# Mixture-of-experts and gated delta attention in one program: one merged head block, a store in steps, scanned counts, and the triangular inversion's 64x64 products interleaved one unit ahead

## The chip, the cores and the metric

The program runs on one core of one Trainium2 chip. The metric is the device time of one execution in microseconds. Everything is float32. Engines: PE (matrix products), PEld (its weight loads), DVE (vector), ACT (scalar), POOL (GpSimd), SP (the engine that issues most DMAs here). Each runs its own list of instructions in order and waits on semaphores.

## The reference

Eight sequences of 256 tokens with 256 features (T = 2048 tokens, 16 row tiles of 128) go through three residual parts. `norm` is a layer norm without weights.

```python
x = x + 0.5 * ffn(norm(x))     # router: softmax over 8 experts, 2 best; each expert 256 -> 896 -> 256,
                               # h = silu(x @ w1) * (x @ w3), out = h @ w2, mixed by the router's weights
x = x + attn(norm(x))
x = x + 0.5 * ffn(norm(x))

# attn: qkvz = x @ W_qkvz (16 key heads, 32 value heads, 128 wide); q, k, v through a causal
# convolution of 4 taps and silu; q and k of unit length; g = -exp(A_log)*softplus(a + dt_bias), beta = sigmoid(b)
def step(state, inp):
    qt, kt, vt, gt, bt = inp
    state = state * jnp.exp(gt)[..., None, None]
    pred = jnp.einsum('bhk,bhkv->bhv', kt, state)
    delta = (vt - pred) * bt[..., None]
    state = state + kt[..., None] * delta[..., None, :]
    return (state, jnp.einsum('bhk,bhkv->bhv', qt, state))
# then core * rsqrt(mean(core^2)) * norm_weight * silu(z), and @ W_out
```

## The kernel before

**Expert parts** (`build_ffn`, twice). `build_norm` makes the normalised rows and their transposes. A chain of small DVE instructions ranks the rows among the experts: `before` is the running count per expert, made by 16 additions one behind the other (L337), `base` the first tile of each expert, made by 8 more (L344). POOL then scatters 32 times 128 rows to `rows_in`, the expert matmuls run over 39 row tiles, and a last block gathers 32 times 128 rows from `rows_out` (POOL, L616) while DVE adds them to `x` (L627). `Pools.end_part` clears the part's semaphores on POOL in a block of its own; a block begins and ends with a barrier of all engines. `build_out` stores `x` (2 MB) with one DMA.

**Head of the attention.** `build_norm` again, then `attention_tables`: 32 small products with `W_ba` (L718; a product is two instructions in the trace, here and elsewhere), a `partition_broadcast` on POOL (L710), and a chain of DVE and ACT instructions that makes the decay tables. The weights of the first head are loaded when the block behind it begins (L1001 to L1004).

**The attention** is worked in 64 units: 16 key heads, and for each 4 units of two sequences (`idx(u)` counts them, `u[1]` is the place within the head). The linear recurrence is done in chunks of 128 tokens; each chunk needs the inverse of a 128x128 triangular matrix, for 8 (chunk, value head) pairs in a unit. Its 32x32 diagonal blocks are inverted on DVE for a whole head at once (`blocks`, in 16 pieces over 4 units), stored to DRAM by `blocks_out` (L1076) and loaded back by `load_c` and `load_t`. The rest is done on PE: `inv_x(32)` and `inv_n` with 32x32 products (L1226, L1227, L1240 to L1242), `inv_x(64)` with eight 64x64 products (L1230) into `inv_bank[0]`, partitions 64 to 127, and `inv_last` with eight (L1250) into `inv_bank[1]`, partitions 0 to 63. ACT copies the result to `invT`, which `solve` reads.

`walk` writes the program of each engine out: it runs over iterations i from -11 to 66, and in each over the steps in the order of a table by hand (one for the filling, one for the steady stretch, one for the draining). A step works on unit i + `STAGE[step]`, so that a unit's steps lie up to 14 iterations apart: projections of q and k at 11, `turn`, `products`, `scan`, `mix` and `spill` at 10, `blocks` at 5, `blocks_out` and the projections of v and z at 1, the inversion at 0, `solve` and `state` at -1, the output at -3. The filling table holds while no v is projected (10 iterations), the draining one when no q and k are left to project (14).

`blocks` piece 0 of a head overwrites `w_up`, so DVE waits until `blocks_out` of the head before has landed: `at_least(dve, s["blocks_stored"], 32 * kh)`. It stands near the start of DVE's list in an iteration. `project` writes a bank that DVE's `conv_qk` (L1467) must have read. `turns` transposes v and waits for both halves of it to be gated, which follow DVE's `conv_v`.

## Time and profile before

| what | value |
|---|---|
| median of 3 runs | 3226.09 us (3223.53 to 3227.19) |
| the profiled execution | 3226.4 us, of which the span from first to last instruction is 3224.7 us |
| mean granted clock of PE | 0.928 |
| busy in the span | PE 86%, PEld 63%, DVE 60%, ACT 43%, POOL 21% |
| first expert part, until its last product row is copied | 0 to 506.4 us |
| gather, norm and tables ahead of the attention's main block | 509.4 to 612.4 us |
| attention's main block | 612.4 to 2667.8 us |
| second expert part, gather and store | 2673.7 to 3224.7 us |

Busy shares are averages over stages. Times in rows count from the span's start. A row of a window: start:end, length, busy us (instructions) of PE, PEld, DVE, ACT, POOL, granted clock, DMA share, GB/s; for one line's instructions their busy time alone. In brackets: the engine's idle time before, and what ended it.

### The profile page before, as it was taken

What the parts mean: (1) busy time and instruction counts of PE and PEld (TensorE: products, weight loads), DVE (VectorE), ACT (ScalarE), POOL (GpSimd) and SP (SyncE); (2) the same over time, 40 slices, a digit from 0 to 9 for tenths busy, and PEclk for the clock granted to TensorE, in tenths of its full rate; (3) what the DMA queues carried; (4) which work ended last, traced back from release to release, by engine and by line L of the source; (5) the groups of instructions that cost most, each with busy time, mean ns of one, the idle gap of its engine ahead of it and who ended that gap; (6) DMA issues with size and microseconds to landing.
All of it is one profiled execution on the core that took longest, in us unless ns stands there. A gap on an engine that the chain in (4) does not pass through costs nothing. (4 is left out here: it accounts for less than half of the span.)

```text
span 3224.7 us, 58916 instructions
## 1 busy us (share of the span) xinstructions
PE 2757.1 (86%) x19218; PEld 2040.5 (63%) x19219; DVE 1943.3 (60%) x3720; ACT 1380.5 (43%) x4437; POOL 671.4 (21%) x959
## 2 busy tenths in 40 slices
PE   2699992556999999999999999999999983699992
PEld 2366661433677777777777777777777772366661
DVE  3122223478898898798798898898886544122222
ACT  0111110233566666566566566666665550111110
POOL 3100004132122222222222222222221112200003
PEclk7799996677999999999999999999999996799996
DMA  5122201145544544544544544545543312122202
GB/s 183 44 94 95 96 26 57 48 149 159 171 141 148 169 151 140 166 152 136 169 152 136 172 150 144 168 146 161 151 130 102 104 46 90 48 95 90 98 27 85
DMA packets 371258, 385.86 MB, mean 120 GB/s; under 512 B 214980, under 2 KB 285508, under 8 KB 371012
## 3 DMA queue, kind: packets, MB, share of 16 engines
q1 hardware_dynamic: 356420, 321.82, 32.6%
q0 software_dynamic: 14592, 60.83, 5.4%
q8 instruction: 146, 2.39, 0.3%
q14 instruction: 100, 0.82, 0.1%
HBM read 239.03 MB, written 143.52 MB: 119 GB/s over the span
## 5 line engine op out<-in xcount | busy, mean ns | idle before, releaser
L480 PE MATMUL f_ps_up<-f_wbuf,f_xgT 128*128 x1248 | 499.1, 543 | 5.4 <-issue 3.4
L575 DVE TENSOR_TENSOR f_h<-f_h,f_ps_up 128x448 f32<-128x448 f32 x156 | 97.0, 621 | 555.0 <-ACT f_h L549 555.0
L549 ACT ACTIVATE f_h<-f_ps_up 128x448 f32<-128x448 f32 x156 | 84.8, 544 | 635.0 <-PE f_ps_up L480 635.0
L480 PEld LDWEIGHTS f_ps_up<-f_wbuf,f_xgT 128*128 128x128 f32 x1248 | 231.2, 192 | 189.1 <-issue 184.8
L1156 PE MATMUL at_bank<-xnT,at_w_qk 128*128 128x512 f32 x512 | 273.9, 664 | 63.6 <-DVE at_qk L1467 57.6
L1467 DVE SCALAR_TENSOR_TENSOR at_qk<-at_bank,at_taps_qk,at_qk 128x510 f32<-128x510 f32 (+2 forms) x384 | 285.0, 744 | 60.9 <-ACT at_qk L1341 51.5
L1467 DVE SCALAR_TENSOR_TENSOR at_vT<-at_bank,at_taps_v,at_vT 128x510 f32<-128x510 f32 (+2 forms) x384 | 280.6, 744 | 36.4 <-ACT at_vT L1348 27.3
L1321 PE MATMUL at_bank<-at_w_out,at_yT 128*128 128x256 f32 x1024 | 260.1, 399 | 37.8 <-issue 31.5
L502 PE MATMUL f_ps_y<-f_wbuf,f_hT 128*128 x1092 | 248.8, 380 | 1.6 <-DVE f_hT L579 1.6
L1169 PE MATMUL at_bank<-xnT,at_w_vz 128*128 128x512 f32 x512 | 235.1, 602 | 15.6 <-DVE at_qk L1467 11.9
L1727 POOL TENSOR_SCALAR at_small<-at_small 128x4 f32<-128x4 f32 x64 | 18.3, 285 | 1089.2 <-ACT at_squares L1375 1089.2
L1321 PEld LDWEIGHTS at_bank<-at_w_out,at_yT 128*128 128x128 f32 x1024 | 193.0, 199 | 68.2 <-issue 34.3
L1181 PE MATMUL at_bank<-at_w_vz,xnT 128*128 128x256 f32 x1024 | 233.7, 381 | 1.8 <-DVE at_vT L1467 1.8
L502 PEld LDWEIGHTS f_ps_y<-f_wbuf,f_hT 128*128 128x128 f32 x1092 | 201.7, 190 | 26.9 <-issue 2.8
L1181 PEld LDWEIGHTS at_bank<-at_w_vz,xnT 128*128 128x128 f32 x1024 | 188.8, 190 | 27.6 <-DVE at_vT L1467 3.4
L1341 ACT ACTIVATE at_qk<-at_bank,at_taps_qk 128x512 f32<-128x512 f32 x128 | 86.9, 688 | 260.9 <-DMA mt_kept<-at_mt_made 142.5
L1156 PEld LDWEIGHTS at_bank<-xnT,at_w_qk 128*128 128x128 f32 x512 | 95.3, 206 | 152.9 <-issue 133.9
L1169 PEld LDWEIGHTS at_bank<-xnT,at_w_vz 128*128 128x128 f32 x512 | 98.2, 193 | 114.4 <-issue 110.8
L210 POOL DMA_DIRECT2D f_wbuf<-in_L_ffn_w_dram x48 | 39.3, 832 | 575.1 <-PE f_ps_y L502 556.8
L1375 ACT ACTIVATE at_squares<-at_bank 128x128 f32<-128x128 f32 x512 | 134.9, 291 | 42.6 <-PE at_bank L1192 41.9
L1444 ACT ACTIVATE at_junk<-at_y 128x128 f32<-128x128 f32 x512 | 150.7, 315 | 1.1 <-DVE at_y L1644 1.1
L1492 DVE TENSOR_TENSOR_SCAN at_decay<-at_steps_e,at_diag_b 128x1024 f32<-128x1024 f32 x64 | 149.9, 2342 | 0.0
(216 smaller groups left out, 5570.4 us busy)
## 6 DMA issues: line engine op xcount, KB each, us to landing
f_wbuf<-in_L_ffn_w_dram POOLq DMA_DIRECT2D x48, 896.0 KB, 8.0
at_steps_e<-steps_kept SPq DMA_DIRECT2D x64, 512.0 KB, 6.0
pt_kept<-at_pt_made SPq DMA_DIRECT2D x64, 512.0 KB, 3.1
mt_kept<-at_mt_made SPq DMA_DIRECT2D x64, 512.0 KB, 4.5
at_mt<-mt_kept SPq DMA_DIRECT2D x64, 512.0 KB, 5.1
at_pt<-pt_kept SPq DMA_DIRECT2D x64, 512.0 KB, 4.8
qk_kept<-at_qk SPq DMA_DIRECT2D x64, 256.0 KB, 3.0
ks_kept<-at_ks_made SPq DMA_DIRECT2D x64, 256.0 KB, 2.1
```

The costliest lines, as they stand in the source:

```text
L480: last = te.matmul(ps_up[hf][w][:, 0:MH], xgT[b][:, k, :], wbuf[:, bass.ds(off + (w * WSIZE + k * M + hf * MH), MH)], start=(k == 0), stop ...
L502: last = te.matmul(ps_y[:, 0:D], hT[b][:, j, :], wbuf[:, bass.ds(off + (2 * WSIZE + j * D), D)], start=(j == 0), stop=(j == MJ - 1))
L575: v.tensor_tensor(part, part, ps_up[hf][1][:, 0:MH], ALU.mult).then_inc(h_ready, 1)
L1156: last = te.matmul(proj_bank[ct][:], w_qk[u[0] % 2][:, k, ct * P:(ct + 1) * P], xnT[:, k, UT * u[1]:UT * u[1] + UT], start=(k == 0), stop= ...
L1169: last = te.matmul(proj_bank[v][:], w_vz[:, k, v * P:(v + 1) * P], xnT[:, k, UT * u[1]:UT * u[1] + UT], start=(k == 0), stop=(k == KD - 1))
L1181: last = te.matmul(proj_bank[half][:, 256 * t:256 * t + 256], xnT[:, k, bass.ds(UT * u[1] + P * (2 * half + t), P)], w_vz[:, k, 2 * P:4 * ...
L1321: last = te.matmul(proj_bank[half][:, 256 * t:256 * t + 256], yT[:, 2 * (2 * half + t) + v, :], w_out[:, v, :], start=(v == 0), stop=(v == ...
L1341: sc.activation(channels(u, ct), proj_bank[ct][:], ACT.Copy, scale=taps_qk[u[0] % 2][:, ct, 3:4]).then_inc(s["acc_qk"], 1)
L1375: last = sc.activation(squares[:, t, :], src[:, P * t:P * t + P], ACT.Square, accum_out=small[two(u)][:, 4 * a + t:4 * a + t + 1])
L1444: last = sc.activation(junk[:, n, :], y[two(u)][:, n, :], ACT.Square, accum_out=osum[two(u)][:, n:n + 1])
L1467: ins = v_.scalar_tensor_tensor(out=dst[:, :, back:], in0=src[:, :, 0:SEQ - back], scalar=taps[:, 3 - back:4 - back], in1=dst[:, :, back:] ...
L1492: v_.tensor_tensor_scan(decay[:].rearrange("p n m -> p (n m)"), steps_e[:], diag_b[:].rearrange("p n m -> p (n m)"), 0.0, ALU.mult, ALU.ad ...
```

## The change

1. The gather of the first expert part, the norm and the tables become one block, `attention_front`, in four groups of four row tiles. POOL issues two groups of gathers, the broadcast, and then alternates between a group's scale and the next gathers; DVE adds, takes moments and shifts; PE transposes and projects group by group; ACT makes all the copies. SP issues the first head's loads in this block. `end_part` of the first expert part now stands between its experts and this block, that of the second one ahead of the last gathers.
2. `build_combine_and_store` stores `x` in 8 pieces of two row tiles, each when its additions are done.
3. The counts are made by two scans in place of 16 and 8 additions.
4. `inv_x` and `inv_n` move to stage 1. The eight 64x64 products of `inv_last` of unit u are issued between the eight of `inv_x(64)` of unit u+1; `inv_last` as a step of its own is left for the last unit. `invT` gets a third buffer, `xb` becomes `xb32` and `xb64`.
5. The stages from the projections of q and k down to `blocks_out` move up by one, so `walk` runs from -12 to 66: 11 filling iterations, 15 draining ones. All orders within an iteration are new.
6. `diag` writes into `decay`, and the scan works in place; `diag` waits for both mixes of the unit before.

```diff
-                        link(v.tensor_tensor(before[:, t + 1, :], before[:, t, :], totals[:, t, :], ALU.add))
-
-                    link(v.tensor_scalar(tiles_i[:], before[:, NT, :], float(P - 1), None, ALU.add))
+                    link(v.tensor_copy(totals[:], ps_rank[:, 1].rearrange("p t e -> p e t")))
+                    link(v.tensor_tensor_scan(reached_by[:].rearrange("p e t -> p (e t)"), carry[:].rearrange("p e t -> p (e t)"),
+                                              totals[:].rearrange("p e t -> p (e t)"), 0.0, ALU.mult, ALU.add))
+
+                    v.tensor_tensor(totals[:], reached_by[:], totals[:], ALU.subtract).then_inc(chain, 1)
+                    n[0] += 1
+                    link(v.tensor_scalar(tiles_i[:], reached_by[:, :, NT - 1], float(P - 1), None, ALU.add))
                     link(v.tensor_scalar(tiles_i[:], tiles_i[:], 7, None, ALU.arith_shift_right))
                     link(v.tensor_copy(tiles_f[:, 0:E], tiles_i[:]))
-                    link(v.memset(base[:, 0:1], 0.0))
-                    for e in range(E):
-                        link(v.tensor_tensor(base[:, e + 1:e + 2], base[:, e:e + 1], tiles_f[:, e:e + 1], ALU.add))
-
-                    link(v.tensor_tensor(slots[:], before[:, 0:NT, :], ps_rank[:, 0], ALU.add))
+                    link(v.tensor_tensor_scan(base[:, 1:E + 1], c["ones"][:, 0:E], tiles_f[:, 0:E], 0.0, ALU.mult, ALU.add))
+
+                    link(v.tensor_tensor(slots[:], totals[:].rearrange("p e t -> p t e"), ps_rank[:, 0], ALU.add))
...
+            def _(sp):
+                rows = out.rearrange("b (c p) d -> p (b c) d", p=P)
+                for g in range(NT // 2):
+                    sp.wait_ge(added, 4 * g + 4)
+                    sp.dma_start(rows[:, 2 * g:2 * g + 2, :], x[:, 2 * g:2 * g + 2, :]).then_inc(c["out_stored"], 16)
+                sp.wait_ge(c["out_stored"], 16 * (NT // 2))
 
...
+                def gather(group):
+                    for n in range(8 * group, 8 * group + 8) if pending else ():
+                        t, k = n // 2, n % 2
+                        at_least(pool, added, n - ring + 1)
+                        nc.gpsimd.indirect_dma_start(
+                            out=yg[n % ring][:], out_offset=None, in_=rows_out,
+                            in_offset=bass.IndirectOffsetOnAxis(ap=slot_of[:, t, k:k + 1], axis=0),
+                        ).then_inc(gathered[n % ring], 16)
+
+                def scale(group):
+                    part = slice(4 * group, 4 * group + 4)
+                    pool.wait_ge(moments_done, 4 * group + 4)
+                    nc.gpsimd.tensor_scalar(rstd[:, part], mv[:, part, 1], LN_EPS, None, ALU.add).then_inc(rstd_done, 1)
+                    pool.wait_ge(rstd_done, 2 * group + 1)
+                    nc.gpsimd.tensor_tensor(rstd[:, part], rstd[:, part], c["minus_half"][:, part], ALU.pow).then_inc(rstd_done, 1)
+
+                gather(0)
+                gather(1)
                 pool.wait_ge(loaded, 48)
                 nc.gpsimd.partition_broadcast(row_all[:].rearrange("p a n -> p (a n)"),
                                               rows[:].rearrange("p a n -> p (a n)"), P).then_inc(spread, 1)
+                for group in range(4):
+                    scale(group)
+                    if group < 2:
+                        gather(group + 2)
...
+                def add(group):
+                    for i in range(8 * group, 8 * group + 8) if pending else ():
+                        t, k = i // 2, i % 2
+                        dve.wait_ge(gathered[i % ring], 16 * (i // ring + 1))
+                        at_least(dve, added, i)
+                        v.scalar_tensor_tensor(out=x[:, t, :], in0=yg[i % ring][:], scalar=weight_of[:, t, k:k + 1],
+                                               in1=x[:, t, :], op0=ALU.mult, op1=ALU.add).then_inc(added, 1)
+
+                def moments(group):
+                    part = range(4 * group, 4 * group + 4)
+                    if pending:
+                        dve.wait_ge(added, 8 * group + 8)
+                    for t in part:
+                        v.bn_stats(stats[:, t, :], x[:, t, :]).then_inc(stats_done, 1)
+                    for t in part:
+                        dve.wait_ge(stats_done, t + 1)
+                        v.bn_aggr(mv[:, t, :], stats[:, t, :]).then_inc(moments_done, 1)
+
+                def shift(group):
+                    dve.wait_ge(moments_done, 4 * group + 4)
+                    dve.wait_ge(rstd_done, 2 * group + 2)
+                    for t in range(4 * group, 4 * group + 4):
+                        v.tensor_scalar(xn[:, t, :], x[:, t, :], mv[:, t, 0:1], rstd[:, t:t + 1],
+                                        ALU.subtract, ALU.mult).then_inc(xn_ready, 1)
...
+
+                for group in range(4):
+                    add(group)
+                    moments(group)
+                    if group:
+                        shift(group - 1)
+                shift(3)
+                dve.wait_ge(spread, 1)
...
 STAGE = {
-    "load_qk": 11, "proj_qk": 11, "conv_qk": 11, "gate_qk": 11,
-    "load_steps": 10, "turn": 10, "ks": 10, "scales": 10, "diag": 10, "products": 10, "scan": 10, "mix": 10, "spill": 10,
-    "blocks_in": 6, "blocks": 5, "low": 5,
-    "blocks_out": 1, "load_c": 1, "load_t": 1,
+    "load_qk": 12, "proj_qk": 12, "conv_qk": 12, "gate_qk": 12,
+    "load_steps": 11, "turn": 11, "ks": 11, "scales": 11, "diag": 11, "products": 11, "scan": 11, "mix": 11,
+    "spill": 11,
+    "blocks_in": 7,
+    "blocks": 6, "low": 6,
+    "blocks_out": 2, "load_c": 2, "load_t": 2,
     "load_vz": 1, "proj_v": 1, "conv_v": 1, "gate_v": 1, "z": 1, "z_gate": 1, "turns": 1, "turn_copies": 1,
-    "load_d": 0, "inv_x": 0, "inv_n": 0, "inv_last": 0,
-    "solve": -1, "weigh": -1, "state": -1, "copy_state": -1, "on_state": -1, "from_state": -1, "output": -1, "join": -1, "lift": -1,
-    "norm": -2, "norm_scale": -2, "shape": -2, "y_turn": -3, "y_copy": -3, "project": -3, "add": -3,
-    "load_wo": -3, "out_weights": -3,
+    "inv_x": 1, "inv_n": 1,
...
+                def last_of(u, n):
+                    return te.matmul(inv_bank[1][0:64, 64 * n:64 * n + 64], xb64[64:P, n, :], invT[idx(u) % 3][64:P, n, 64:P],
+                                     start=True, stop=True)
...
+                        return
+
+                    pe.wait_ge(s["n_copied"], idx(u) + 1)
+                    pe.wait_ge(s["n_copied_t"], idx(u) + 1)
+                    at_least(pe, s["x_ready"], 2 * idx(u))
+                    for n in range(N8):
+                        if idx(u):
+                            last = last_of(shift(u, -1), n)
+                            if n == N8 - 1:
+                                last.then_inc(s["last_psum"], 1)
+                        x64 = te.matmul(inv_bank[0][64:P, 64 * n:64 * n + 64], m[0:64, n, 64:P], w[0:64, n, :], start=True, stop=True)
+                    x64.then_inc(s["x_psum"], 1)
...
                 def inv_last(u):
+                    if idx(u) < UNITS - 1:
+                        return
                     pe.wait_ge(s["x_ready"], 2 * idx(u) + 2)
                     pe.wait_ge(s["n_copied_t"], idx(u) + 1)
+                    at_least(pe, s["invT_ready"], idx(u))
                     for n in range(N8):
-                        last = te.matmul(inv_bank[1][0:64, 64 * n:64 * n + 64], xb[64:P, n, :], invT[two(u)][64:P, n, 64:P],
-                                         start=True, stop=True)
+                        last = last_of(u, n)
...
                     dve.wait_ge(s["steps_loaded"], 16 * (idx(u) + 1))
                     dve.wait_ge(s["diag_ready"], idx(u) + 1)
-                    at_least(dve, s["mt_ready"], idx(u))
-                    at_least(dve, s["pt_ready"], idx(u))
                     v_.tensor_tensor_scan(decay[:].rearrange("p n m -> p (n m)"), steps_e[:],
-                                          diag_b[:].rearrange("p n m -> p (n m)"), 0.0, ALU.mult, ALU.add).then_inc(s["decay_ready"], 1)
+                                          decay[:].rearrange("p n m -> p (n m)"), 0.0, ALU.mult, ALU.add).then_inc(s["decay_ready"], 1)
 
...
                     pool.wait_ge(s["b_ready"], idx(u) + 1)
-                    at_least(pool, s["decay_ready"], idx(u))
+                    at_least(pool, s["mt_ready"], idx(u))
+                    at_least(pool, s["pt_ready"], idx(u))
                     apart()
...
-SP_ORDER = (("blocks_out",), ("load_qk",), ("load_d",), ("load_c",), ("load_steps",), ("load_t",), ("blocks_in",),
-            ("load_wo",), ("load_vz",), ("spill",))
+SP_ORDER = (("load_wo",), ("blocks_out",), ("load_c",), ("load_d",), ("load_steps",), ("load_t",), ("blocks_in",),
+            ("spill",), ("load_qk",), ("load_vz",))
```

**PE, a steady iteration.** Before, from the second v projection on (`at_bank2` and `at_bank3` are the two `inv_bank`s; L1230 is `inv_x(64)`, L1203 `products`, L1181 `z`, L1213 `turns`, L1250 `inv_last`, L1297 `output`):

```order
L1169 MATMUL at_bank1<-xnT,at_w_vz 128x512 x2
L1230 MATMUL at_bank2<-at_inv0,at_mt0 64x64 x8
L1203 MATMUL at_bank6<-at_qk0 128x128 x4
L1203 MATMUL at_bank4<-at_qk0 128x128 x4
L1181 MATMUL at_bank0<-at_w_vz,xnT 128x256 x4
L1181 MATMUL at_bank1<-at_w_vz,xnT 128x256 x4
L1213 MATMUL at_bank5<-ident,at_vT 128x128 x4
L1213 MATMUL at_bank7<-ident,at_vT 128x128 x4
L1250 MATMUL at_bank3<-at_invT0,at_xb 64x64 x8
L1297 MATMUL at_bank5<-at_wv,at_pt1 128x128 x4
L1297 MATMUL at_bank6<-at_wv,at_pt1 128x128 x4
```

After, first the place where the 64x64 products now stand (L1427 is `y_turn`, L1407 `on_state`, L1327 `inv_last`'s products, L1350 those of `inv_x(64)`):

```order
L1427 MATMUL at_bank5<-ident,at_y1 128x128 x4
L1407 MATMUL at_bank6<-at_state,at_late_qk1 128x256 x2
L1407 MATMUL at_bank7<-at_state,at_late_qk1 128x256 x2
L1327 MATMUL at_bank3<-at_invT0,at_xb64 64x64
L1350 MATMUL at_bank2<-at_inv1,at_mt1 64x64
```

The last two rows alternate eight times. Later in the same iteration, after `project` (L1278 is the v projection, L1387 `solve` of the second chunk, L1312 `products`, L1290 `z`, L1322 `turns`, L1419 `output`):

```order
L1278 MATMUL at_bank1<-xnT,at_w_vz 128x512 x2
L1387 MATMUL at_bank4<-at_vr0,at_invT1 128x128 x4
L1312 MATMUL at_bank6<-at_qk0 128x128 x4
L1312 MATMUL at_bank4<-at_qk0 128x128 x4
L1290 MATMUL at_bank0<-at_w_vz,xnT 128x256 x4
L1322 MATMUL at_bank5<-ident,at_vT 128x128 x4
L1290 MATMUL at_bank1<-at_w_vz,xnT 128x256 x4
L1322 MATMUL at_bank7<-ident,at_vT 128x128 x4
L1419 MATMUL at_bank5<-at_wv,at_pt0 128x128 x4
L1419 MATMUL at_bank6<-at_wv,at_pt0 128x128 x4
```

Both groups of eight stand together ahead of `project`; `solve` of the second chunk stands behind the v projections, and the first `turns` ahead of the second `z`.

**DVE, the iteration in which `blocks` of a new head begins.** Before, from `inv_x(32)` (L1626) on: L1592 is the first write of `w_up`, L1467 `conv_qk`, L1635 `from_state`, L1659 `add`:

```order
L1626 TENSOR_SCALAR at_xb<-at_bank2 128x8x32
L1592 TENSOR_SCALAR at_w_up<-at_up 128x16
L1542 TENSOR_TENSOR at_terms<-at_w_up,at_up 128x8 x8
L1546 TENSOR_REDUCE at_half_way<-at_terms 128x32
L1467 SCALAR_TENSOR_TENSOR at_qk0<-at_bank0,at_taps_qk1,at_qk0 128x2x255
L1467 SCALAR_TENSOR_TENSOR at_qk0<-at_bank0,at_taps_qk1,at_qk0 128x2x254
L1467 SCALAR_TENSOR_TENSOR at_qk0<-at_bank0,at_taps_qk1,at_qk0 128x2x253
L1635 SCALAR_TENSOR_TENSOR at_vr0<-at_bank6,at_t_minus_start,at_vr0 128x128 x4
```

After (L1748 is `inv_x`; L1712 the first write of `w_up`, L1675 and L1681 the second piece of `blocks`, L1589 `conv_qk`):

```order
L1712 TENSOR_SCALAR at_w_up<-at_up 128x16
L1662 TENSOR_TENSOR at_terms<-at_w_up,at_up 128x8 x8
L1666 TENSOR_REDUCE at_half_way<-at_terms 128x32
L1675 TENSOR_TENSOR at_terms<-at_half_way,at_w_up 128x8 x8
L1681 TENSOR_REDUCE at_w_up<-at_terms 128x2x2 x8
L1589 SCALAR_TENSOR_TENSOR at_qk0<-at_bank0,at_taps_qk1,at_qk0 128x2x255
L1589 SCALAR_TENSOR_TENSOR at_qk0<-at_bank0,at_taps_qk1,at_qk0 128x2x254
L1589 SCALAR_TENSOR_TENSOR at_qk0<-at_bank0,at_taps_qk1,at_qk0 128x2x253
L1589 SCALAR_TENSOR_TENSOR at_qk0<-at_bank1,at_taps_qk1,at_qk0 128x2x255
L1589 SCALAR_TENSOR_TENSOR at_qk0<-at_bank1,at_taps_qk1,at_qk0 128x2x254
L1589 SCALAR_TENSOR_TENSOR at_qk0<-at_bank1,at_taps_qk1,at_qk0 128x2x253
L1748 TENSOR_SCALAR at_xb64<-at_bank2 64x512
```

The second piece of `blocks` moved ahead of `conv_qk`, and `from_state` behind both filters and behind the copy of the 64x64 products.

**SP, around `blocks_out`.** Before (L1069 is `blocks_in`, L1030 and L1032 `load_vz`, L1052 to L1058 `spill`, L1076 `blocks_out`):

```order
L1069 DMA at_up<-mt_kept 32x32x32 x4
L1030 DMA at_w_vz<-in_L0_attn_W_qkvz_dram 128x512 x2
L1032 DMA at_taps_v<-in_L0_attn_conv_weight_dram 128x4 x2
L1052 DMA qk_kept<-at_qk0 512x1x128
L1054 DMA ks_kept<-at_ks_made 128x512
L1056 DMA pt_kept<-at_pt_made 128x1024
L1058 DMA mt_kept<-at_mt_made 128x1024
L1076 DMA blocks_kept<-at_w_up 128x1024
L1076 DMA blocks_kept<-at_w_low 128x1024
L1106 DMA at_pt1<-pt_kept 128x1024
```

After (L1181 is `blocks_in`, L1164 to L1170 `spill`, L1188 `blocks_out`):

```order
L1181 DMA at_up<-mt_kept 32x32x32 x4
L1164 DMA qk_kept<-at_qk0 512x1x128
L1166 DMA ks_kept<-at_ks_made 128x512
L1168 DMA pt_kept<-at_pt_made 128x1024
L1170 DMA mt_kept<-at_mt_made 128x1024
L1188 DMA blocks_kept<-at_w_up 128x1024
L1188 DMA blocks_kept<-at_w_low 128x1024
L1201 DMA at_mt0<-mt_kept 128x1024
L1204 DMA at_inv0<-blocks_kept 32x8x32 x3
```

`load_vz`, which waits for the z projection, no longer stands ahead of the `spill` that `blocks_out` follows; `load_c` (L1201), which waits for the landing of `blocks_out`, stands ahead of `load_d` (L1218).

## Rows read from the trace of the kernel before

**Rows 1.** Windows: a steady unit, one at a head's start, a draining one.

```profile
1175.00:1203.70 28.70, 28.70 (x250) 22.53 (x249) 26.15 (x37) 18.71 (x64) 7.15 (x11) 1.00 0.47 148
1351.10:1387.80 36.70, 31.71 (x251) 24.46 (x250) 25.08 (x73) 19.07 (x65) 6.88 (x11) 0.91 0.56 181
2523.70:2548.30 24.60, 23.06 (x224) 18.36 (x219) 10.80 (x23) 13.55 (x41) 2.09 (x3) 1.00 0.36 102
```

**Rows 2.** Timeline of PE in that steady unit (start, duration, line).

```profile
1187.71 1.88 PE L1169 MATMUL at_bank<-xnT,at_w_vz 128*128 128x512 f32 x4
1189.52 1.14 PE L1230 MATMUL at_bank<-at_inv,at_mt 64*64 64x64 f32 x16
1190.60 2.05 PE L1203 MATMUL at_bank<-at_qk 128*128 128x128 f32 x16
...
1200.85 0.21 PE L1226 MATMUL at_bank<-at_inv,at_mt 32*32 32x32 f32 x1
...
1201.48 0.70 PE L1156 MATMUL at_bank<-xnT,at_w_qk 128*128 128x512 f32 x1
```

**Rows 3.** Timeline at a head's start (SP issues, DVE, PE).

```profile
1351.58 1.21 SPq L1076 DMA_DIRECT2D blocks_kept<-at_w_low  x1
...
1358.55 0.18 DVE L1592 TENSOR_SCALAR at_w_up<-at_up 128x16 f32<-128x16 f32 x1 [8.97 <-DMA blocks_kept<-at_w_low]
...
1362.25 2.04 PE L1321 MATMUL at_bank<-at_w_out,at_yT 128*128 128x256 f32 x4 [4.03 <-issue]
```

**Rows 4.** What ended DVE's idle time before the first write of `w_up`, all heads.

```profile
  DMA blocks_kept<-at_w_low: 104.8, 15
```

**Rows 5.** Windows, one line each: L1276 (8 in a unit), L1492 (one).

```profile
935.40:2345.40 1410.00, 49.55 (x376) 49.17 (x375) 0.99 0.50 154
2399.00:2622.40 223.40, 10.43 (x72) 8.71 (x72) 1.00 0.34 95
...
650.90:711.90 61.00, 9.13 (x4) 0.72 0.50 155
```

**Rows 6.** Timeline of the attention's head.

```profile
509.38 1.04 POOL L616 DMA_INDIRECT f_yg<-rows_out,f_slot_of  x1 [115.27 <-PEq L609]
...
548.25 0.95 POOL L616 DMA_INDIRECT f_yg<-rows_out,f_slot_of  x1 [0.30 <-issue]
...
551.03 0.48 DVE L627 SCALAR_TENSOR_TENSOR x<-f_yg,f_weight_of,x 128x256 f32<-128x256 f32 x1 [0.79 <-DMA f_yg<-rows_out,f_slot_of]
554.64 5.32 DVE L173 BATCH_NORM_STATS2 at_stats<-x 128x6 f32<-128x256 f32 x16 [3.13 <-PEq L81]
...
561.62 2.94 POOL L168 TENSOR_TENSOR at_rstd<-at_rstd,minus_half 128x16 f32<-128x16 f32 x1
...
576.44 13.92 PE L718 MATMUL tab_ps_ba<-tab_w_ba,xnT 128*128 128x64 f32 x64 [3.62 <-DMA tab_rows<-in_L_attn_dt_bias_dram]
579.82 0.37 POOL L710 PARTITION_BROADCAST tab_row_all<-tab_rows  x1 [15.25 <-issue]
...
593.00 0.43 DVE L769 TENSOR_SCALAR tab_m<-tab_a 128x512 f32<-128x512 f32 x1
...
616.08 4.26 PE L1156 MATMUL at_bank<-xnT,at_w_qk 128*128 128x512 f32 x5 [6.05 <-DMA at_taps_qk<-_L_attn_conv_weight_dram]
```

**Rows 7.** Timeline of the second routing; what ended POOL's idle time, by tile `rows_in`.

```profile
2715.13 3.18 DVE L337 TENSOR_TENSOR f_before<-f_before,f_totals 128x8 f32<-128x8 f32 x16
...
2719.09 1.52 DVE L344 TENSOR_TENSOR f_base<-f_base,f_tiles_f 128x1 f32<-128x1 f32 x8
...
  DMA rows_in<-zeros: 26.6, 1
```

**Rows 8.** Timeline of the last addition; page, DMA issues (KB, us to landing).

```profile
3213.24 0.48 DVE L627 SCALAR_TENSOR_TENSOR x<-f_yg,f_weight_of,x 128x256 f32<-128x256 f32 x1 [0.72 <-DMA f_yg<-rows_out,f_slot_of]
...
out_dram<-x SPq DMA_DIRECT2D x1, 2048.0 KB, 7.5
```

**Rows 9.** Page, costly groups: the filter of v.

```profile
L1467 DVE SCALAR_TENSOR_TENSOR at_vT<-at_bank,at_taps_v,at_vT 128x510 f32<-128x510 f32 (+2 forms) x384 | 280.6, 744 | 36.4 <-ACT at_vT L1348 27.3
```

363 lines of the change are left out of this document (202 added, 161 removed).

## The prediction

> **What bounds the kernel now.** I went from the windows by stage to the timeline of PE, and from there to what the other engines wait for. In the steady stretch a unit takes 28.7 us and PE is busy for all 28.70 of them at full granted clock, DVE for 26.15, ACT for 18.71 [rows 1]. So in that stretch an instruction taken from PE is worth its whole length, but only until DVE, which has 2.55 us free, becomes the bound. The timeline shows what may be saved: eight 64x64 products (16 instructions) run from 1189.52 to 1190.60, 1.08 us, 67 ns each [rows 2]. The grouping by `state` (8 instructions a unit) gives 47 units in 1410.0 us, 30.0 each [rows 5], where 28.7 would make 1349. The 61 us over belong to the 12 head starts inside, 5.1 each. One of them lasts 36.70 us, with 31.71 busy: 5.0 idle and, at a granted clock of 0.91, 3.0 of slower work [rows 1]. There the store of `w_low` is issued at 1351.58, DVE gets on only at 1358.55 after 8.97 idle, and PE stands 4.03 at `project` [rows 3]. All 15 such waits of DVE sum to 104.8 us, 7.0 each [rows 4]. A draining unit takes 24.8 us (9 in 223.4) [rows 5], PE busy in 23.06 of 24.6 [rows 1]. A filling one takes 61.0 / 4 = 15.25 [rows 5]. Outside the main block only single chains count: the head [rows 6], the second routing [rows 7] and the end [rows 8].
>
> **The change, part by part.** The sum is made against the profiled execution, 3226.4 us, 1.7 of it outside the span; the median, 3226.1, is the same within 0.3.
>
> *A, the head: -20.* Before, gathers run from 509.38 to 548.25 for 32, so (548.25 - 509.38) / 31 = 1.254 us apart; the last addition ends at 551.51, 3.3 after the last gather's start; `tab_m` is made at 593.00 [rows 6]. After: `end_part` now precedes. The gap from 551.51 to 554.64 is 3.1 for block ends and `end_part` [rows 6]; one block end stood there before too, so I take 2.4 and start at 511.8. 16 gathers (20.1), the broadcast (its row gives 0.37, but from 576.44, when its operands had landed, to its end are 3.75; I take that, 3.8), scale (0), 8 gathers (10.0), scale (1), 8 gathers. A scale on 4 columns is bounded by a quarter of 2.94 and 2.94 [rows 6]; I take 1.6 with the semaphore step. The last gather thus starts at 511.8 + 20.1 + 3.8 + 1.6 + 10.0 + 1.6 + 8.8 = 557.7, the last addition ends at 561.0. Moments of four tiles 5.32 / 4 = 1.3 and 0.4 for the aggregates (562.7), scale 1.6, shift 1.4 (about as the statistics), transposes and copies 2.6 (565.8 to 568.4), projection 13.92 / 4 = 3.5, splits 1.2: `tab_m` at 573.1, 19.9 earlier. Bounds -13 and -25 (broadcast at 0.37, projection in half that time).
>
> *B, first loads: -3.4.* PE's first product stands at 616.08 behind a load, in a block that begins at 612.4 [rows 6]. The loads now lie beside the tables, 40 us of work. Without that cover: 0.
>
> *C, counts: -4.1.* 3.18 and 1.52 go, and 0.2 of small writes [rows 7]. A scan of 1024 elements takes 9.13 / 4 = 2.28 us [rows 5], so one of 128 about 0.3, one of 8 about 0.1; with copy and subtraction 0.8. In the first routing POOL waited 26.6 for `zeros` [rows 7], and that wait takes up the gain: 0.
>
> *D, the end: -5.0.* From the last addition (3213.72) to the span's end are 11.0 us: a new block, then a store of 2 MB that lands in 7.5 [rows 8]. Now 256 KB are left, which land in something between 7.5 / 8 = 0.9 and 7.5; I take 2.5 and 0.4 for the issue. `end_part` moves ahead of the gathers and costs its 3.1 there: -11.0 + 2.9 + 3.1. Bounds -7 and 0.
>
> *E, the interleaving: -66.* What two groups of eight cost together is bounded by 1.08 us (the second is free) and 2.15 (as now). The nearest row is the pair of 32x32 products L1226 and L1227, which lie in different rows of the array: 32 instructions from 1200.85 to 1201.48, 0.63 us, 39 ns for a pair [rows 2]. A pass of 512 columns takes (1189.52 - 1187.71) / 4 = 0.4525 us, 0.884 ns a column [rows 2]; so one of 32 columns is 28 ns and some 10, one of 64 is 57 and 10. The pair costs what one costs, so the 64x64 pair should be 67 ns too, its two groups lie in different halves of the rows and in different banks. That is -1.07 for each unit bound by PE: 51 steady and 11 draining ones, -66. Bounds 0 and -70.
>
> Were the 10 ns beyond the columns the loads of one's own row group, laid bare, a mixed order would lose them too: 16 x 57 ns = 0.91 for both, a gain of 1.24 a unit, -77, and 3125 in all. But the 32-wide pair of two groups has its 10 ns as well, so the trace speaks against. The Trainium skill ("TensorE: Matmul & The Clock Gate", Part 3: Packing small matmuls — row/col tiling) gives this rule: a weight load overlaps products in flight only when its row group differs. By that rule it would be 3125, by the rows 3136.
>
> *F, one stage more: +11.* One filling iteration (15.25) and one draining (24.8 - 1.1) come, one steady (28.7 - 1.1) goes: +11.3. Bounds +5 and +15.
>
> *G, head starts: -20.* `blocks_out` no longer stands behind `load_vz`, and 7.0 us from issue to landing stay [rows 3]. I expect it issued some 1.5 to 3 us earlier in the iteration, and DVE's wait shorter by that. But the second piece of `blocks` now precedes `conv_qk`, for which `project` waits, and the iteration is shorter. So PE's loss goes from 5.1 to about 3.4: 12 x -1.7 = -20. Bounds 0 and -61.
>
> *H, new small waits: +17.* `turns` now stands before the second `z`, behind two v filters of three instructions at 280.6 / 384 = 0.73 us [rows 9], 4.4, and with ACT's copy and gate some 5.7. From the point where the filters can start PE has half a v projection (0.9), the second `solve` (1.0, half of what the same count of `products` takes), `products` 2.05 [rows 2] and the first `z` (8 passes of 256 columns at 0.884 ns, 1.8): 5.8, just enough. Where DVE is held by a piece of `blocks` it is late by some tenths, and `project` in the last unit of a head by 0.6 to 0.8. I put 1.4 on a head's four units, 12 times. Without any: 0. If each of 51 units lost 1.0: +50.
>
> Part 6 (one tile less) costs nothing: POOL is busy 7.15 of 28.70 [rows 1].
>
> Sum: -20 - 3.4 - 4.1 - 5.0 - 66 + 11.3 - 20 + 17 = -90, 3226.4 - 90 = **3136**.
>
> **The rivals.**
> - *Loads laid bare* in today's groups of eight, and hidden in the mixed order: E is -77, 3125; the 10 ns of the mixed 32-wide pair stand against it; 0.05. The page of the Trainium skill named under E has this as a rule.
> - *No overlap*: the 64x64 products alternate at 67 ns each, E is 0. Against it stands the 39 ns pair. 3136 + 66 = 3202; 0.08.
> - *DVE binds.* PE would need 27.63, DVE is busy 26.15 [rows 1] and runs in order behind copies of ACT. If 1.0 us of waits a unit appears at `turns`, `project` or `solve`, then 47 x 1.0 on top: 3183; 0.15.
> - *Head starts vanish*: `blocks_kept` lands before DVE asks, or PE has enough to do meanwhile. G is -61 in place of -20 and H is 0: 3136 - 41 - 17 = 3078. For it: DVE's wait need only fall below what PE has queued; against: 7.0 of landing stay. 0.14.
> - *Slower.* PE waits at `turns` in each unit for DVE's filters of v long enough for its granted clock to fall, as at 1351.10, where 5.0 idle brought 3.0 more [rows 1]. It decides from 90 / 51 = 1.8 us a unit; with 2.6 idle and 1.6 by the clock it is 4.2 x 51 = +214, less the 17 of H: 3136 + 197 = 3333. Against it: the chain of 6.3 fits within tenths. 0.04.
> - *The change doesn't do what it says*: the interleaved order runs as before and new waits eat the ends' gains, 3226; 0.02.
>
> **How the numbers follow.** Forecast as summed: 0.52, its own range 3105 to 3165 (E 0 to -4, G ±15, H -17 to +15, A ±6). What can be told from no change is about 0.2%, 6.5 us. Faster takes all but the last two rivals: 0.94; same 0.02; slower 0.04. The range 3080 to 3200 leaves out the last two (0.06), half of "head starts vanish" (0.07), half of "no overlap" (0.04) and the tail of "DVE binds" (0.02): 0.19.
>
> **What the profile after would show.** A and B: `tab_m` near 573, the first product of the main block within 0.5 us of its start. C: about 0.8 for the scans. D: some 3 us behind the last addition. E: 32 instructions of 64x64 in about 1.1 us; if 2.1, no overlap. F: 15.25 longer filling. G: DVE's waits before `w_up` summing to some 70 to 85 in place of 104.8, a unit at a head start near 34 to 35 us. H: PE's idle time before `turns` and `project` in tenths in the other units. A steady unit of 27.6 with PE at 100% confirms the base; one above 28.3 makes the forecast wrong by 35 us or more, and so does a head start without PE idle.

## The result

| kernel | median us | lowest to highest | ratio to before, 95% interval |
|---|---|---|---|
| before | 3224.81 | 3223.12 to 3227.19 | |
| changed | 3184.63 | 3181.33 to 3191.12 | 0.9875 [0.9858, 0.9891] |

The change takes 40.2 us off; 90 were forecast. The time lies in the range given (3080 to 3200), but 50 of the 90 us are missing. The span is 3184.5 us, the mean granted clock 0.923.

Windows of the changed kernel, with columns as in [rows 1]: an ordinary steady unit, one at a head start, eight draining ones.

```profile
1264.50:1292.20 27.70, 27.68 (x249) 21.52 (x248) 26.00 (x37) 18.93 (x65) 6.23 (x11) 1.00 0.44 140
1319.90:1356.00 36.10, 29.73 (x249) 22.66 (x248) 25.25 (x73) 18.82 (x65) 7.93 (x12) 0.95 0.54 182
2381.70:2569.60 187.90, 175.72 (x1729) 139.44 (x1729) 110.90 (x241) 108.12 (x320) 24.50 (x28) 1.00 0.35 101
```

The ordinary unit fell from 28.7 to 27.7 us with PE busy in all of it, as forecast. The draining one fell from 24.8 to 187.9 / 8 = 23.5. The unit at a head start takes 36.1: PE is idle for 6.4, and the mean granted clock is 0.95. The grouping by `state` over the same 47 units as in [rows 5]:

```profile
939.30:2333.10 1393.80, 49.55 (x376) 49.18 (x375) 0.98 0.51 155
```

47 units in 1393.8 us. Of these 34 are ordinary (27.76 on average, from the starts of `state` in the trace) and the last one is shorter already (26.2), so the 12 head starts take (1393.8 - 34 x 27.76 - 26.2) / 12 = 35.3 each. Before they took (1410.5 - 35 x 28.74) / 12 = 33.7, where 1410.5 is the length from start to start. So half of the saving in the ordinary units was eaten at the head starts: 47 units gained 17 us in place of the 53 of the forecast's E, G and H.

Timeline of PE in that ordinary unit, the 64x64 products (L1327 and L1350 alternate), and in the unit of [rows 2] the last of the eight before the change:

```profile
1270.19 0.27 PE L1327 MATMUL at_bank<-at_invT,at_xb 64*64 64x64 f32 x1
1270.20 0.27 PE L1350 MATMUL at_bank<-at_inv,at_mt 64*64 64x64 f32 x1
1270.30 0.22 PE L1327 MATMUL at_bank<-at_invT,at_xb 64*64 64x64 f32 x1
1270.30 0.22 PE L1350 MATMUL at_bank<-at_inv,at_mt 64*64 64x64 f32 x1
1270.35 0.22 PE L1327 MATMUL at_bank<-at_invT,at_xb 64*64 64x64 f32 x1
...
1271.12 0.22 PE L1350 MATMUL at_bank<-at_inv,at_mt 64*64 64x64 f32 x1
1271.27 0.33 PE L1301 MATMUL at_bank<-ident,at_qk 128*128 128x128 f32 x1
```

```profile
1190.45 0.22 PE L1230 MATMUL at_bank<-at_inv,at_mt 64*64 64x64 f32 x1
1190.60 0.38 PE L1203 MATMUL at_bank<-at_qk 128*128 128x128 f32 x1
```

In the changed kernel a pair starts every 58 ns but for the first gap (0.11 us), and from the first start to the next instruction both groups take 1.08 us. Before, one group took the same 1.08, and its own instructions started 58 ns apart as well, with 0.11 behind the first and 0.15 behind the last.

Timeline of the changed kernel at a head start (the iteration in which `state` begins at 1319.9), to be held against [rows 3]:

```profile
1322.10 1.22 SPq L1188 DMA_DIRECT2D blocks_kept<-at_w_low  x1
...
1325.19 0.69 ACT L1463 ACTIVATE at_qk<-at_bank,at_taps_qk 128x512 f32<-128x512 f32 x1 [3.39 <-DMA mt_kept<-at_mt_made]
...
1327.12 0.24 PE L1327 MATMUL at_bank<-at_invT,at_xb 64*64 64x64 f32 x1 [1.45 <-ACT at_inv L1524]
...
1328.91 0.18 DVE L1712 TENSOR_SCALAR at_w_up<-at_up 128x16 f32<-128x16 f32 x1 [9.78 <-DMA blocks_kept<-at_w_low]
...
1333.94 0.77 PE L1443 MATMUL at_bank<-at_w_out,at_yT 128*128 128x256 f32 x1 [3.80 <-issue]
```

DVE idles 9.78 us, more than the 8.97 of before, and over all heads 117.8 us against 104.8 [rows 4]. The store of `w_low` is issued 2.2 us behind the start of `state`; before it was 0.9 behind. Of PE's 6.4 idle, 5.3 are two stops: one of 3.80 at `project` as before, and a new one of 1.45 ahead of the 64x64 products (L1327), because ACT has the copy of `inv_n` (L1524) queued behind its part of `conv_qk` (L1463), which waits 3.39 us for the landing of a spill.

Timeline of the merged head block, to be held against [rows 6]:

```profile
511.69 1.04 POOL L735 DMA_INDIRECT tab_yg<-rows_out,slot_of  x1 [117.18 <-POOLq L81]
...
537.67 0.37 POOL L750 PARTITION_BROADCAST tab_row_all<-tab_rows  x1 [5.90 <-issue]
...
545.20 0.25 POOL L743 TENSOR_SCALAR tab_rstd<-tab_mv 128x4 f32<-128x4 f32 x1 [7.16 <-issue]
...
567.36 0.94 POOL L735 DMA_INDIRECT tab_yg<-rows_out,slot_of  x1 [0.30 <-issue]
...
580.53 6.93 PE L774 MATMUL tab_ps_ba<-tab_w_ba,xnT 128*128 128x64 f32 x32
...
588.41 0.43 DVE L874 TENSOR_SCALAR tab_m<-tab_a 128x512 f32<-128x512 f32 x1
...
607.94 2.04 PE L1265 MATMUL at_bank<-xnT,at_w_qk 128*128 128x512 f32 x2 [2.20 <-PEq L716]
```

The gathers begin at 511.69, as forecast (511.8). But around the `partition_broadcast` POOL idles 5.90 us ahead and 7.16 behind it, where I had put 3.8 for all. The two gaps are alike in three other kernels with this order (5.8 to 6.0 and 7.1 to 7.2). So the last gather starts at 567.36 in place of 557.7, 9.7 later. `tab_m` is made at 588.41 and not at 573.1, so another 5.6 lie behind the last gather. The largest part of them is on PE: behind the last transposes it has the products of two groups to do, 6.93 us (L774), where I had put those of one, 3.5. The first product stands at 607.94: 8.1 earlier than before, of which 4.6 are the head and 3.5 the early loads.

The end, to be held against [rows 8], and the counts, against [rows 7]:

```profile
3181.44 0.48 DVE L633 SCALAR_TENSOR_TENSOR x<-end_yg,weight_of,x 128x256 f32<-128x256 f32 x1 [0.20 <-issue]
3181.95 0.37 SPq L642 DMA_DIRECT2D out_dram<-x  x1
```

```profile
2683.23 0.42 DVE L338 TENSOR_TENSOR_SCAN f_reached_by<-f_carry,f_totals 128x128 f32<-128x128 f32 x1
...
2684.51 0.18 DVE L346 TENSOR_TENSOR_SCAN f_base<-ones,f_tiles_f 128x8 f32<-128x8 f32 x1
```

The last addition ends 2.6 us before the span does. From the last copy of the second expert part to the end, the gather with it, it took 49.6 us in place of 56.0: -6.4. The scans take 0.42 and 0.18; the chain from L334 to L353 took 7.9 before (L337 to L355 now 3.8), 4.1 less. Of this 3.0 reach the end of the expert part (501.0 us before and 498.0 now, from the last addition of the attention to the last copy). Against it stands the way from the first scatter to the first instruction of PE there, 49.4 us in place of 47.4. These 2.0 lie between SP's issue of the first rows' load and that instruction, and why the load is slower stays open.

### The profile page after: what moved, and what is told of

It is laid out like the page before. It is cut to its first block and busy times, and to the rows that moved or that the text cites. A ratio compares the mean times of both kernels' runs of the same rounds, so it can differ in the third digit from the quotient of the medians.

```text
span 3184.5 us, 58919 instructions
## 1 busy us (share of the span) xinstructions
PE 2707.1 (85%) x19218; PEld 1991.8 (63%) x19219; DVE 1935.7 (61%) x3676; ACT 1383.8 (43%) x4441; POOL 663.7 (21%) x966
## 5 line engine op out<-in xcount | busy, mean ns | idle before, releaser
L1589 DVE SCALAR_TENSOR_TENSOR at_qk<-at_bank,at_taps_qk,at_qk 128x510 f32<-128x510 f32 (+2 forms) x384 | 280.9, 744 | 48.2 <-ACT at_qk L1463 39.1
L1589 DVE SCALAR_TENSOR_TENSOR at_vT<-at_bank,at_taps_v,at_vT 128x510 f32<-128x510 f32 (+2 forms) x384 | 280.5, 744 | 36.4 <-ACT at_vT L1470 27.4
L1443 PE MATMUL at_bank<-at_w_out,at_yT 128*128 128x256 f32 x1024 | 266.2, 409 | 35.3 <-issue 32.7
L1290 PE MATMUL at_bank<-at_w_vz,xnT 128*128 128x256 f32 x1024 | 245.2, 383 | 8.1 <-DVE at_vT L1589 8.1
L1443 PEld LDWEIGHTS at_bank<-at_w_out,at_yT 128*128 128x128 f32 x1024 | 202.2, 207 | 67.0 <-issue 37.8
L1278 PE MATMUL at_bank<-xnT,at_w_vz 128*128 128x512 f32 x512 | 233.5, 597 | 4.3 <-issue 2.2
L1290 PEld LDWEIGHTS at_bank<-at_w_vz,xnT 128*128 128x128 f32 x1024 | 185.7, 191 | 29.6 <-DVE at_vT L1589 9.3
L1470 ACT ACTIVATE at_vT<-at_bank,at_taps_v 128x512 f32<-128x512 f32 x128 | 88.0, 688 | 190.9 <-PE at_bank L1278 190.9
L1278 PEld LDWEIGHTS at_bank<-xnT,at_w_vz 128*128 128x128 f32 x512 | 97.4, 192 | 102.6 <-issue 98.4
L1612 DVE TENSOR_TENSOR_SCAN at_decay<-at_steps_e,at_decay 128x1024 f32<-128x1024 f32 x64 | 148.6, 2322 | 0.0
```

The lines of the kernel that those rows point to most:

```text
L1278: last = te.matmul(proj_bank[v][:], w_vz[:, k, v * P:(v + 1) * P], xnT[:, k, UT * u[1]:UT * u[1] + UT], start=(k == 0), stop=(k == KD - 1))
L1290: last = te.matmul(proj_bank[half][:, 256 * t:256 * t + 256], xnT[:, k, bass.ds(UT * u[1] + P * (2 * half + t), P)], w_vz[:, k, 2 * P:4 * ...
L1443: last = te.matmul(proj_bank[half][:, 256 * t:256 * t + 256], yT[:, 2 * (2 * half + t) + v, :], w_out[:, v, :], start=(v == 0), stop=(v == ...
L1470: sc.activation(channels(u, ct), proj_bank[v][:], ACT.Copy, scale=taps_v[:, v, 3:4]).then_inc(s["acc_v"], 1)
L1589: ins = v_.scalar_tensor_tensor(out=dst[:, :, back:], in0=src[:, :, 0:SEQ - back], scalar=taps[:, 3 - back:4 - back], in1=dst[:, :, back:] ...
L1612: v_.tensor_tensor_scan(decay[:].rearrange("p n m -> p (n m)"), steps_e[:], decay[:].rearrange("p n m -> p (n m)"), 0.0, ALU.mult, ALU.add ...
```

## The experiments

Two theories on the head starts. **Theory L**: PE's loss comes from DVE's wait for the landing of `blocks_kept`. **Theory A**: it comes from ACT's wait for the landing of the spill, with `inv_n` queued behind. And on the head block, **theory K**: the broadcast brings 13 us of idle POOL of its own. Where it matters the length of a head start is given, worked out as above from the window over the same 47 units. All kernels are the changed one with the edit shown, but for the two that start from the kernel before. The interval of each ratio is 0.0013 to 0.0019 to each side, 4 to 6 us. Differences to the changed kernel are those of the medians; by the ratios they come out 4 to 5 us lower in the first four runs, and within 2 us in the others.

**The products apart** (`e5_apart`).

```diff
-                    for n in range(N8):
-                        if idx(u):
-                            last = last_of(shift(u, -1), n)
+                    for n in range(N8 if idx(u) else 0):
+                        last = last_of(shift(u, -1), n)
...
+                    for n in range(N8):
                         x64 = te.matmul(
```

> The changed kernel with its eight 64x64 products of inv_last issued first and the eight of inv_x(64) behind them, at the same place of PE's list, in place of alternating. All else is as changed. If the alternation is what shortened the unit from 28.7 to 27.7 us, the two groups take 2.15 us again in place of about 1.1, a unit of the steady stretch takes 28.7 to 28.8, and 63 units give +60 to +68: about 3248. If the shorter unit comes from the new orders and the stages alone, the time stays at 3185 within 5.

Measured: 3213.84 us, ratio 0.995 [0.9935, 0.9966], 29 more than the changed kernel and not 60 to 68. An ordinary unit takes 28.38 us on average, not 28.7 to 28.8. Alternation shortens the unit, but by 0.62 and not by 1.07. Timeline of PE in this kernel:

```profile
1280.64 0.96 PE L1327 MATMUL at_bank<-at_invT,at_xb 64*64 64x64 f32 x13
1281.40 0.27 PE L1350 MATMUL at_bank<-at_inv,at_mt 64*64 64x64 f32 x1
1281.45 0.22 PE L1327 MATMUL at_bank<-at_invT,at_xb 64*64 64x64 f32 x1
1281.50 0.22 PE L1350 MATMUL at_bank<-at_inv,at_mt 64*64 64x64 f32 x1
...
1281.62 0.92 PE L1350 MATMUL at_bank<-at_inv,at_mt 64*64 64x64 f32 x13
1282.47 0.66 PE L1301 MATMUL at_bank<-ident,at_qk 128*128 128x128 f32 x4
```

Both groups, written one behind the other, take from 1280.64 to 1282.47, 1.83 us; two separate groups took 1.08 and 1.07 in the kernel before. The starts show why: products of `inv_x(64)` (L1350) begin at 1281.40, when three of `inv_last` are still to start, though they stand behind them in the list. At the seam the two are mixed without being written so, and mere neighbourhood gives 0.3 of the 1.07. Alternation gives the rest of it on the two groups (1.83 to 1.08); 0.62 of these 0.75 reach the unit.

**blocks_out early** (`e1_out_early`).

```diff
-    "blocks_out": 2, "load_c": 2, "load_t": 2,
+    "blocks_out": 3, "load_c": 2, "load_t": 2,
...
-SP_ORDER = (("load_wo",), ("blocks_out",), ("load_c",), ("load_d",), ("load_steps",), ("load_t",), ("blocks_in",),
+SP_ORDER = (("load_wo",), ("load_c",), ("load_d",), ("load_steps",), ("load_t",), ("blocks_out",), ("blocks_in",),
```

> The changed kernel with blocks_out one stage earlier and directly ahead of blocks_in on SP's list, so that it is issued when the last piece of blocks is transposed (at 1314.2 in the head start near 1320) and not behind blocks_in and spill (1320.9). Theory L (PE's loss at head starts comes from DVE's wait for the landing of blocks_kept): DVE's wait of 9.8 us falls to about 3, project no longer waits, a head start falls from 36.1 to about 32: -3 to -4 for each of 12, about 3140 to 3150. Theory A (it comes from ACT, which waits for the landing of the spill before conv_qk, with inv_n queued behind it): the spill is now 2.4 us later, the products L1327 wait for inv_n 3.5 to 4 us in place of 1.5, and the time is 3185 to 3215.

(The same move is made in the orders of the filling and the draining stretch.) What ended DVE's idle time before `w_up`, all heads, in the changed kernel and in this one, and PE's before L1327 in this one's 47 units:

```profile
  DMA blocks_kept<-at_w_low: 117.8, 15
...
  DMA at_up<-mt_kept: 40.4, 10
  issue: 19.2, 5
...
  ACT at_inv L1524: 55.3, 12
```

Measured: 3174.53 us, 0.983 [0.9817, 0.9844]; 10 less than the changed kernel, and not the 35 to 45 of theory L. DVE's wait at that place, now mostly for `up`, falls from 117.8 to 59.6 us over all heads, but a head start takes 35.0 in place of 35.3. PE's stops at `project` are gone (0.7 us over the 47 units), and in their place stands the one ahead of the 64x64 products, 55.3 us in 12 stops, as theory A had it. Each theory was right on its own wait and wrong that it was the only one: the wait moved.

**inv_n first on ACT** (`e2_inv_n_first`).

```diff
-ACT_ORDER = (("weigh", 0), ("norm",), ("copy_state",), ("conv_qk", 0), ("inv_n",),
+ACT_ORDER = (("weigh", 0), ("norm",), ("copy_state",), ("inv_n",), ("conv_qk", 0),
```

> The changed kernel with ACT's copy of inv_n ahead of its conv_qk of q. Only conv_qk waits for the landing of the spill; inv_n's operands are there 3.6 us earlier. Theory A: the wait of PE before L1327 (13.6 us over 12 head starts, and the clock that goes with it) vanishes: -15 to -35, 3150 to 3170. Theory L: PE gets to project earlier by as much and waits there for as much longer, since conv_qk on DVE stays behind the landing of blocks_kept: 3185 within 5. In the three other units of a head nothing changes in either.

Measured: 3191.31 us, 0.9883 [0.9866, 0.9899]: no gain (7 more than the changed kernel, the intervals overlap), as theory L had it. A head start takes 35.9. The stop ahead of L1327 is gone, the one at `project` grew from 34.8 to 53.9 us over the 47 units.

**blocks_in and blocks_out early** (`e8_in_and_out_early`). As `e1_out_early`, and:

```diff
-                    at_least(sp, s["low_ready"], 2 * u[0])
+                    at_least(sp, s["block_step"], STEPS * (u[0] - 1) + sum(COUNTS[:7]))
...
+SP_ORDER = (("load_wo",), ("load_c",), ("load_d",), ("load_steps",), ("blocks_in",), ("load_t",), ("blocks_out",),
+            ("spill",),
```

In words: `blocks_in` waits for the piece of `blocks` that reads `up` last, no longer for the transposition, and stands ahead of `load_t`; `blocks_out` stands behind `load_t`.

> As the run with blocks_out early, and blocks_in moved ahead of load_t, with its wait set to the piece of blocks that reads up last (piece (1,2)) in place of the last piece. So neither blocks_in nor blocks_out holds the spill by more than 2.4 us behind the transposition. Theory L: 3140 to 3150 again. Theory A: spill about as in the changed kernel, so 3180 to 3190. Both causes together, one behind the other: lower than each of the two single edits, 3100 to 3140.

Measured: 3106.44 us, 0.9619 [0.9605, 0.9633]: 78 less than the changed kernel, where each of the two edits above gave 10 or nothing. Head starts take 29.7 us and the granted clock stays at 1.00 in the whole stretch. So both waits hold PE, one behind the other, and both hang on the moment at which SP gets past `blocks_in`. What held `blocks_in`? It waits for `low`, POOL's transposition of the last blocks. POOL's timeline in the changed kernel, in the iteration ahead of the same head start:

```profile
1308.51 0.24 POOL L1878 TENSOR_SCALAR at_osum<-at_osum 128x8 f32<-128x8 f32 x1
...
1309.31 1.67 POOL L1880 TENSOR_TENSOR at_osum<-at_osum,minus_half 128x8 f32<-128x8 f32 x1 [0.18 <-POOL at_osum L1879]
1310.93 0.63 POOL L1833 COPY at_w_low<-at_w_up 128x256 f32<-128x256 f32 x1
1311.50 2.64 POOL L1834 COPY at_w_low<-at_w_up 128x256 f32<-128x256 f32 x1
```

`low` (L1833, L1834) now stands behind `norm_scale` (L1878 to L1880), which takes 2.4 us; and its second copy takes 2.64 us in place of 0.63 (0.628 median before), since it now starts while DVE is in its scan (L1612, 1311.24 to 1313.71). What matters is which of the two starts first (to some 0.02 us). In the kernel before, too, the second copy and the scan overlap, but at each of the 12 head starts the copy began 0.17 to 0.19 us ahead of the scan: it took 0.63, and the scan 2.60 in place of its usual 2.28. So the transposition ends 5.8 us ahead of `state`, before the change 9.4. The forecast did not look at POOL's list, in which this one pair was swapped.

**low ahead of norm_scale** (`g1_low_ahead`), the order of before:

```diff
-POOL_ORDER = (("scales",), ("diag",), ("out_weights",), ("norm_scale",), ("low",))
+POOL_ORDER = (("scales",), ("diag",), ("out_weights",), ("low",), ("norm_scale",))
```

> The changed kernel with one pair of POOL's list swapped in the steady stretch: low (the transposition of the last blocks) stands ahead of norm_scale again, as before the change. The transposition should end about 2 to 4 us earlier in the iteration before a head start (it ended 5.9 us ahead of state, before the change 9.5), blocks_in goes out as much earlier, and with it spill and blocks_out, of which the spill is then held by mt (ready 4.9 ahead of state). Theory L and theory A both: both landings come about 2 us earlier, a head start falls from 35.4 to about 33: -20 to -35, 3150 to 3165. Rival P (norm_scale, now late, delays y and so PE at y_turn or project as much): 3185 within 5.

Measured: 3116.23 us, 0.9659 [0.9643, 0.9675]: 68 less by one swapped pair, twice what was expected. Its timeline of POOL, and its grouping by `state`:

```profile
1296.82 0.65 POOL L1834 COPY at_w_low<-at_w_up 128x256 f32<-128x256 f32 x1
1297.42 0.26 POOL L1878 TENSOR_SCALAR at_osum<-at_osum 128x8 f32<-128x8 f32 x1
```

```profile
941.10:2270.40 1329.30, 49.53 (x377) 49.17 (x376) 1.00 0.53 163
```

The copy takes 0.65 again and ends 10.2 us ahead of `state`, 4.4 earlier; DVE's waits before `w_up` sum to 74.9 us in place of 117.8, and a head start takes (1329.3 - 34 x 27.76 - 26.2) / 12 = 29.9 us. Over the 47 units PE's idle time fell from 62.3 to 23.1 us, and the time at the lower level of the granted clock (1.2 in place of 2.4 GHz) from 61.4 to 6.8, which at half speed is 27 us: 66 in all, for a window 64.5 shorter. The expectation had counted the landing alone. The expectation's rival P, a late `norm_scale` that holds PE, did not show.

**The same swap the other way, in the kernel before** (`h5_before_low_last`).

```diff
-POOL_ORDER = (("scales",), ("diag",), ("out_weights",), ("low",), ("norm_scale",))
+POOL_ORDER = (("scales",), ("diag",), ("out_weights",), ("norm_scale",), ("low",))
```

> The kernel before the change with the one pair of POOL's list swapped the other way: norm_scale ahead of low in the steady stretch. There norm_scale waits for ACT's squares until 1341.7 in the iteration ahead of the head start near 1351 and takes 3.7, so the transposition would end at about 1347 in place of 1341.3 (5 to 6 us later), and blocks_in, load_vz, spill and blocks_out move back by what of that isn't slack. If the late transposition is what made the head starts of the changed kernel long, they grow here too, from 33.7 to 37 to 40 us: +40 to +75, 3266 to 3300. If the head starts of the changed kernel are long for something else in its orders, nothing here by over 10 us.

Measured: 3276.7 us, 1.015 [1.0136, 1.0164], 48 more than before, in the range expected. Head starts take 37.2. The same swap makes the head starts long in the old kernel too, if by another stop of PE. What ended PE's idle time before `on_state` (L1285) in the 47 units:

```profile
  ACT at_state L1419: 67.0, 12
```

ACT's copy of the state stands in its list behind `conv_qk`, which waits for the landing of the spill, as `inv_n` does in the changed kernel. At `project` only 4.7 us are left, and `low` takes its 0.63, so here the swap acts by the order alone.

**blocks early in the kernel before** (`h4_before_early`): the edits of `e8_in_and_out_early`, fitted to its stages.

> The kernel before the change with blocks_out one stage earlier, directly behind load_t, and blocks_in early, with its wait on piece (1,2). If the wait of DVE for the landing (104.8 us over the heads) and the spill's wait in ACT are what made its head starts 5.0 us longer than 28.75, they fall to 29 to 30: -40 to -55, 3172 to 3186. If something else there holds project, under 10 us.

Measured: 3173.2 us, 0.983 [0.9811, 0.9848]: -55. Head starts take (1355.3 - 35 x 28.74) / 12 = 29.1, nearly an ordinary unit's length (28.7). The kernel before could be made 11 us faster than the changed one (15 by the ratios) by SP's orders and one of its waits alone.

**The second piece of blocks behind the filters** (`g3_piece_behind`).

```diff
-DVE_ORDER = (("inv_x", 32), ("blocks", 0), ("blocks", 1), ("conv_qk", 0), ("conv_qk", 1), ("inv_x", 64), ("add", 0),
+DVE_ORDER = (("inv_x", 32), ("blocks", 0), ("conv_qk", 0), ("conv_qk", 1), ("blocks", 1), ("inv_x", 64), ("add", 0),
```

> The changed kernel with the second piece of blocks on DVE behind both filters of q and k in place of ahead of them. At a head start conv_qk comes 1.35 us earlier after the landing of blocks_kept. If project waits for it at the end of that chain, each of 12 head starts gains 1.0 to 1.35 and its share of the clock: -12 to -25, about 3160 to 3172. If ACT's late conv_qk is what PE waits for in the end (theory A), 3185 within 5.

Measured: 3156.6 us, 0.979 [0.9773, 0.9807]: -28, somewhat more than expected. Head starts fall to 32.1, but an ordinary unit grows from 27.76 to 28.19, with new stops of PE at `turns` and the v projection. Over the 47 units PE is idle nearly as long as in the changed kernel (59.8 us and 62.3), 42 and 60 of it at the head starts; the time at the lower level of the clock fell from 61.4 to 3.4 us. So the greater part of the gain came by the clock, which the expectation had only named.

**The broadcast late** (`g2_broadcast_late`).

```diff
-                pool.wait_ge(loaded, 48)
-                nc.gpsimd.partition_broadcast(...)
                 for group in range(4):
                     scale(group)
                     if group < 2:
                         gather(group + 2)
+                pool.wait_ge(loaded, 48)
+                nc.gpsimd.partition_broadcast(...)
```

> The changed kernel with the partition_broadcast on POOL behind the last scale of the merged head block in place of between the second and the third group of gathers (ACT's exponential of it behind the last copies). Theory K (the broadcast brings 5.9 us of idle POOL ahead of it and 7.2 behind it, 13.5 with itself, and this holds the gathers): gathers end 13.5 us earlier; the broadcast is then done about 6 us behind the last scale, beside shift, transposes, copies and products, and the second half of 7.2 lies beside the tables: tab_m at about 575 to 577 in place of 588.4, -11 to -13.5. Rival W: POOL waits there for something else, the operands or the adds, the gap stays at the same place and tab_m moves by under 1 us.

Measured: 3170.39 us, 0.9831 [0.9814, 0.9849]: -14. Theory K holds (ACT's exponential of the broadcast rows moved behind its last copies with it):

```profile
566.72 0.37 POOL L754 PARTITION_BROADCAST tab_row_all<-tab_rows  x1 [6.05 <-issue]
...
575.14 0.43 DVE L874 TENSOR_SCALAR tab_m<-tab_a 128x512 f32<-128x512 f32 x1
```

The idle time ahead of the broadcast moves with it (6.05 us), and `tab_m` is made 13.3 us earlier. The Trainium skill ("GPSIMD Engine Reference", 2.1 Instruction dispatch) puts the first call of a freshly loaded kernel at about 6 us, with no instruction in the profile: the 5.90 and 6.05 agree in length. What POOL does in the 7.16 behind the broadcast no trace shows. A kernel that loads the rows by DMA in place of the broadcast has no measured time, so it isn't shown that all 13.4 us would go with it.

**Together** (`h1_best`): `e8_in_and_out_early`, `g1_low_ahead` and `g2_broadcast_late`.

> The changed kernel with three edits together: low ahead of norm_scale on POOL, blocks_in and blocks_out early on SP, the broadcast behind the last scale. Head starts were 35.4 us in the changed kernel, 29.8 with low ahead alone, 29.7 with the early blocks alone. If both edits remove the same wait, head starts stay at 29.3 to 29.7 and the time is 3106 less the 13.5 of the broadcast: 3090 to 3095. If each removes a part of its own (theory of two waits one behind the other), head starts fall to 28.3 to 28.8: 3075 to 3085.

Measured: **3075.2 us, 0.9531 [0.9513, 0.9549]**, 109 less than the changed kernel and the best of all. The grouping by `state`, and what ended DVE's idle time before `w_up`:

```profile
915.20:2223.20 1308.00, 49.56 (x377) 49.20 (x376) 1.00 0.55 165
```

```profile
  DMA at_up<-mt_kept: 6.2, 2
```

Head starts take 28.2 us. The wait for `blocks_kept` does not occur any more; each of the two edits on the head starts had taken a part of its own.

**Two undoings on the cured kernels** (`h2_low_apart`: `g1_low_ahead` with the products apart; `h3_best_piece`: `h1_best` with the second piece behind the filters).

> The changed kernel with low ahead of norm_scale (3116 us) and the two groups of 64x64 products one behind the other in place of alternating. With long waits at the head starts the same undoing cost 29 us (0.75 in each unit bound by PE, and some of it given back where PE waits anyhow). If the head starts swallowed a part, the undoing costs more here, since PE waits less: 0.75 in 62 units, +42 to +48, 3158 to 3164. If 29 is all there is: 3145.

> As the kernel with all three edits, with the second piece of blocks on DVE behind both filters. In the changed kernel this gave 28 us: head starts fell by 3.5 us while each ordinary unit grew by 0.4. If it only shortened the chain behind the late landing, then with the landing early nothing is gained at the head starts, and the 0.4 in each of some 36 units stays: +12 to +18 against the kernel with all three edits. If the piece also delays project without the landing, it stays a gain: -5 to -20.

Measured: 3147.7 us (0.9756 [0.9737, 0.9774]), 31 more than `g1_low_ahead`; of the two readings expected, the one with 42 to 48 was wrong. An ordinary unit goes from 27.76 to 28.38 and a draining one from 23.7 to 24.4, while a head start falls from 29.9 to 29.5. So alternation against neighbourhood is worth 0.62 a unit wherever it was tried, and the long head starts did not hide more. And 3096.83 us (0.96 [0.9582, 0.9618]), 22 more than `h1_best` and not 12 to 18: head starts stay at 28.2, the 47 units take 15 more, and 6 more stand ahead of the first `state`. Where the landing is early, the piece ahead of the filters is the better order. Its gain of 28 us in the changed kernel was only that of a shorter chain behind the late landing, with what the clock gave back.

## Why the prediction missed

The steps that failed are two: what `blocks_out` was held by (G, 36 of the 50 us missed, with what E and H had put on the head starts) and the price of the broadcast (A, 15).

- **A, the head (-20)**: -4.6. The step that failed is the price of the broadcast, "I take that, 3.8". It costs POOL 13.4 us (5.90 + 0.37 + 7.16), and it stood between two groups of gathers, on the path: 9.6 of the 15.4 us missed. Of the rest 3.4 are the second group of products behind the last transposes, which the sum took as done. The 15.25 us of idle POOL ahead of it in the kernel before lay beside other work and did not show what of it was its own. Moving it made `tab_m` 13.3 earlier.
- **B (-3.4)**: -3.5. **C (-4.1)**: 4.1 in the chain, 3.0 in the part, with 2.0 lost at the first load behind the scatters, for a reason that is open. **D (-5.0)**: -6.4.
- **E, the interleaving (-66)**: right in mechanism and size where PE is the bound: 28.7 to 27.7 in the 34 ordinary units of the window, 24.8 to 23.5 in a draining one. `e5_apart` shows that it is the order of the products and not the new stages: 0.62 of the 0.98 by alternation, the rest as much as neighbourhood gives. The 12 head starts did not get it, since they aren't bound by PE. Loads laid bare, the rival with 1.24 a unit, is refuted. The 67 ns for each instruction in the prediction were a mean over the whole group; within it they started 58 ns apart before the change too, in one half of the rows, and 64 columns at the 0.884 ns of [rows 2] are 57. So their weight loads cost nothing there, the rule named with this rival in the prediction is not borne out by this group, and the rest of the 1.08 lies behind the first and the last instruction.
- **F (+11)** with E outside the 47 units: forecast as +11.3 and -16, so -5; measured +16.3 from the first product to the first `state`, -4.3 to the window's start, -20.7 from its end to the last `state` and +2.6 behind that: -6. Right.
- **G, head starts (-20)**: with E and H the forecast had put -1.4 on a head start; measured are +1.6, 36 us over the 12, and this is the step that cost most. "I expect it issued some 1.5 to 3 us earlier" rested on `load_vz` alone. What SP waited for was `low`, through `blocks_in`; `low` came 3.6 us later by its place in POOL's list and by its copy starting behind DVE's scan. So the store went out later behind the start of `state`, 1.3 us at the head start shown and 1.9 on average over the 12, DVE waited longer, and ACT's wait for the spill gained a victim (`inv_n`). With that one pair put back, DVE's waits sum to 74.9 us, inside the 70 to 85 forecast, and a head start takes 29.9, 3.8 less than before the change: without the swap G was right in its direction and too small.
- **H (+17)**: in ordinary units nothing was seen beyond 0.2 us in the one behind a head start. At the head starts PE waits 6.0 us before `turns`, 0.5 each, and 5.7 remain in `h1_best`; `project` is held by the landing, and its part of the 17 can't be told from G.

Of the rivals none was what happened. The nearest in sum, "DVE binds" at 3183, is refuted: ordinary units stay at 27.7 with PE busy throughout, and that its number was hit is chance. "Head starts vanish" became true only with the added edits, and at 3075 it lands close to the 3078 worked out for it, with the broadcast's 13 us in it.

## What to carry to other kernels

A step that one DMA queue waits for can be held by any engine: before trusting an earlier issue, follow each wait on that queue to the engine that ends it, and read that engine's list for swaps, also when the engine is idle most of the time. Where two waits lie one behind the other, curing one moves the stop to the other; single edits gave 10 us and none, easing both at once 68 and 78. Price the `partition_broadcast` on GpSimd by the idle time on both sides of it, and keep it off the path.

## What had not been expected of the hardware

Of two neighbouring groups of 64x64 products in different row halves, the second starts before all of the first have started (L1350 at 1281.40 ahead of L1327 at 1281.45): they take 1.83 us for 2.15 without any alternation. A copy of 128x256 on POOL that starts within a scan of DVE takes 2.64 us in place of 0.63 and ends 0.4 us behind it (1314.14 and 1313.71); one that starts 0.18 us ahead of the scan takes its 0.63, and the scan 2.60 in place of 2.28. And stops can cost more than their length: 5.0 us idle brought 3.0 of slower work in one head start of before [rows 1], 6.4 brought 2.0 in one of the changed kernel, and in `e8_in_and_out_early`, with 23 us idle in place of 62 over the 47 units, the time at the lower level was 0 in place of 61 us. The sum of the idle time does not decide it: in `g3_piece_behind` 60 us in shorter stops (one of 3.1, the others under 2) brought 3.4 us at the lower level, where the changed kernel had 13 stops of over 2.
